# First-layer weights as the stationary operand in the expert tiles of a one-core metaformer kernel

## The chip, the cores and the metric

One Trainium2 chip, one core. The metric is the device time in microseconds (us) of one execution. Engines: PE (TensorE; its weight loads are written PEld), DVE (VectorE), ACT (ScalarE), POOL (GpSimd), SP (SyncE, which only issues DMAs here).

## What is computed

The input is 8 images of 64 channels and 16 x 16 pixels. Two blocks follow each other: deformable convolution and LSTM, then deformable convolution and a mixture of experts. The change touches the last part alone:

```
logits = flat @ router_w.T                      # 2048 tokens, 8 experts, the best 2 are taken
h = silu(flat @ w1[e].T) * (flat @ w3[e].T)     # 64 channels -> 682 hidden units
y = h @ w2[e].T                                 # 682 -> 64
out = sum over the two experts of gate * y
```

## The kernel before, in words

The 4096 pairs of token and expert are sorted by expert into 39 tiles of 128 rows (NT = 39); a tile has one expert, whose number the PE reads into a register. 16-bit operands are split into a high and a low float16 part, so each product is two matmuls.

- **POOL** gathers a tile's 128 rows from DRAM with an indirect DMA (fetch, L1195), seven tiles ahead, and scatters a tile's results with another (spread, L1202). In its loop fetch of tile t + 7 stands before spread of tile t, and spread waits for the row sums of DVE.
- **PE** turns the tokens (turn_tokens, L721): high and low parts of the 64 channels lie on 128 partitions. ACT copies that to `xts` (L1087).
- **first** (L724 to L739): for w1 (m = 0) and for w3 (m = 1), two halves of 341 hidden units times two parts. The stationary operand is `xts`, the moving one 341 columns of the weights at an address that hangs on the expert's register, so tokens are on partitions in the result. Eight matmuls a tile.
- ACT applies SiLU to the w1 result (gated, L1095); DVE multiplies it with the w3 result into `htok`, 128 tokens x 682 units of float32 (gated, L1688).
- **turn_hidden** (L741 to L750): six float32 transposes bring the units of `htok` onto partitions, into two banks of PSUM.
- ACT casts these banks to the high float16 part (high, L1104, two pieces), DVE subtracts to get the low part (low, L1697, two pieces).
- **second** (L752 to L767): twelve matmuls, six blocks of 128 units times two parts; the moving operand is w2 at a register address, which both parts of a block share. DVE adds the two halves of the result (rows_out, L1703).

The PE's order is written by hand (L775 to L784): in step t it does first(t), turn_tokens(t + 1), turn_hidden(t - 1), second(t - 2). ACT's order is gated(t), turned_tokens(t + 1), high(t - 1); DVE's is gated(t), low(t - 1), rows_out(t - 2). All waits are semaphores between engines. After the last spread the results are read back, weighted, turned (L787), added and stored.

Of the kernel before, what the change touches and what calls it, by code (L numbers as in the profile page):

```python
# [20 lines left out]
F32 = mybir.dt.float32  # L21
F16 = mybir.dt.float16
# [8 lines left out]
BQ = B // 2  # L31
# [63 lines left out]
def build(nc, x, consts, conv_w, conv_b, sample_w, bn, lstm_u, lstm_v, lstm_b, router, w13, w2, out):  # L95
    with ExitStack() as ctx:
# [3 lines left out]
        def sem(name):  # L100
            return ctx.enter_context(nc.semaphore(name))

        duo = [ctx.enter_context(nc.psum_tensor(f"duo{i}", [P, 1024], F32)) for i in range(2)]
        single = [ctx.enter_context(nc.psum_tensor(f"bank{i}", [P, 512], F32)) for i in range(4, 8)]
        bank = [duo[i // 2][:, i % 2 * 512:i % 2 * 512 + 512] for i in range(4)] + [b[:, :] for b in single]

        tent_c = sb("tent_c", [P, 2, 2, TAPS, 16])
# [93 lines left out]
        ytok = over(st0, 0, [P, 16 * 2 * C]).rearrange("p (g k n) -> p g k n", g=16, k=2)  # L202
        lsel = over(st1, 0, [P, 32 * TILE], F16).rearrange("p (c n) -> p c n", c=32)
        ybuf = over(st1, 0, [P, NP40 * C]).rearrange("p (t c) -> p t c", t=NP40)
        silu = over(st1, 2560, [P, 2 * HID]).rearrange("p (u n) -> p u n", u=2)
        xts = over(st1, 3924, [P, 3 * TILE], F16).rearrange("p (u n) -> p u n", u=3)
        hh = zw[0][:, :, :, :, :].rearrange("p a b c d -> p (a b c d)").rearrange("p (u n) -> p u n", u=3)
        hl = zw[1][:, :, :, :, :].rearrange("p a b c d -> p (a b c d)").rearrange("p (u n) -> p u n", u=3)
        htok = hid[:, :, :].rearrange("p a b -> p (a b)")[:, 0:2 * HP].rearrange("p (u n) -> p u n", u=2)
# [39 lines left out]
        for n in ("ld_const", "ld_mean", "ld_x", "ld_conv", "ld_lstm", "ld_w", "ld_late",  # L249
                  "zero", "bn_a", "bn_d",  # L250
                  "c_max", "c_tr", "c_pow", "c_bc", "c_scale",
                  "w_part", "w_max", "w_tr", "w_pow", "w_bc", "w_scale", "w_fac", "w_high", "w_low", "l_scaled",
                  "l_gi", "l_o", "l_act", "l_oact", "l_c", "l_tc", "l_h", "l_hc", "l_up", "l_res", "l_init", "l_zero", "r_half", "r_seed", "r_newton",
                  "e_pads", "e_conv", "e_om", "e_turn", "e_omt", "e_sig", "e_dist", "e_far", "e_tents", "e_tent",
                  "k_const", "x_turned", "x_centred", "x_square", "x_var", "x_sd", "x_rs", "m_log", "m_high", "m_low", "m_xrow", "m_exp",
                  "m_sm", "m_rank", "m_tot", "m_pos", "m_lane",
                  "m_tab", "m_zero",
                  "m_xtp", "m_xts", "m_h", "m_silu", "m_hid", "m_ht", "m_hh", "m_hl",
                  "m_y", "m_ys", "m_rows", "m_yld", "m_gate", "m_mix", "m_sum", "m_tr",
                  *[f"m_g{k}" for k in range(AHEAD)],  # L260
                  "m_out", "st_out"):
            s(n)
# [64 lines left out]

            return (slice(0, 8), slice(8, 12), slice(12, 16))[q]

        def halves_of(m):  # L330

            return duo[m][:, :].rearrange("p (h n) -> p h n", h=2)[:, :, 0:HID // 2]
# [61 lines left out]
        def _(pe):  # L394
# [321 lines left out]
            def turn_tokens(t):  # L716

                pe.wait_ge(s(f"m_g{t % AHEAD}"), 16 * (t // AHEAD + 1))
                if t > 0:
                    pe.wait_ge(s("m_xts"), t)  # L720
                nc.tensor.transpose(bank[4][:, 0:64].bitcast(F16), xg[:, t, :], ident16[:, :])\  # L721
                    .then_inc(s("m_xtp"), 1)

            def first(t):  # L724

                e = owner_of(t)

                n = HID // 2
                pe.wait_ge(s("m_xts"), t + 1)
                for m in range(2):  # L730
                    if t > 0:
                        pe.wait_ge(s(("m_silu", "m_hid")[m]), t)
                    for half in range(2):
                        for part in range(2):
                            at = 2 * SLOT + part * EW + m * HID + half * n
                            mm = nc.tensor.matmul(duo[m][:, half * 512:half * 512 + n], xts[:, t % 3, :],  # L736
                                                  w16[:, bass.ds(e * SLOT + at, n)],
                                                  start=(part == 0), stop=(part == 1))
                    mm.then_inc(s("m_h"), 1)  # L739

            def turn_hidden(t):  # L741

                pe.wait_ge(s("m_hid"), t + 1)
                for b in range(EB):
                    if t > 0 and b % 4 == 0:
                        pe.wait_ge(s("m_hl"), 2 * t - 1 + b // 4)
                    mm = nc.tensor.transpose(bank[6 + b // 4][:, b % 4 * 128:b % 4 * 128 + 128],  # L747
                                             htok[:, t % 2, b * 128:b * 128 + 128], ident[:, :])
                    if b in (3, EB - 1):
                        mm.then_inc(s("m_ht"), 1)  # L750

            def second(t):  # L752

                e = owner_of(t)

                if t > 0:
                    pe.wait_ge(s("m_ys"), t)
                for b in range(EB):
                    if b % 4 == 0:
                        pe.wait_ge(s("m_hl"), 2 * t + 1 + b // 4)  # L760
                    for part in (hh, hl):
                        mm = nc.tensor.matmul(bank[5][:, 0:2 * C],  # L762
                                              part[:, t % 3, b * 128:b * 128 + 128],
                                              w216[:, bass.ds(e * HP + (2 * HP + b * 128), 128)],
                                              start=(b == 0 and part is hh), stop=(b == EB - 1 and part is hl),
                                              skip_group_check=True)
                mm.then_inc(s("m_y"), 1)  # L767

            pe.wait_ge(s("m_tab"), 1)
            pe.wait_ge(s("w_low"), PAIRS * PAIRK)  # L770
            pe.wait_ge(s("m_zero"), 1)
            pe.wait_ge(s("m_high"), 4)
            loaded = [pe.value_load(words[0:1, k:k + 1], min_val=0, max_val=E ** TPW - 1) for k in range(WORDS)]
            turn_tokens(0)
            for t in range(NT + 2):  # L775
                if t < NT:
                    first(t)
                    if t + 1 < NT:
                        turn_tokens(t + 1)
                if 1 <= t <= NT:  # L780
                    turn_hidden(t - 1)
                if t >= 2:
                    second(t - 2)
            for j in range(8):  # L784
# [9 lines left out]
        def _(act):  # L794
# [287 lines left out]
            def turned_tokens(t):  # L1082

                act.wait_ge(s("m_xtp"), t + 1)
                if t >= 3:
                    act.wait_ge(s("m_h"), 2 * (t - 2))
                nc.scalar.copy(xts[:, t % 3, :], bank[4][:, 0:64].bitcast(F16))\  # L1087
                    .then_inc(s("m_xts"), 1)

            def gated(t):  # L1090

                act.wait_ge(s("m_h"), 2 * t + 1)
                if t >= 2:
                    act.wait_ge(s("m_hid"), t - 1)
                nc.scalar.activation(silu[:, t % 2, :].rearrange("p (h n) -> p h n", h=2), halves_of(0), ACT.Silu, scale=wsc[:, 4:5])\  # L1095
                    .then_inc(s("m_silu"), 1)

            def high(t):

                if t >= 3:  # L1100
                    act.wait_ge(s("m_y"), t - 2)
                for k, (lo, hi) in enumerate(((0, 512), (512, HP))):
                    act.wait_ge(s("m_ht"), 2 * t + k + 1)
                    nc.scalar.copy(hh[:, t % 3, lo:hi], bank[6 + k][:, 0:hi - lo]).then_inc(s("m_hh"), 1)  # L1104

            turned_tokens(0)
            for t in range(NT + 1):
# [9 lines left out]
        def _(gp):  # L1117
# [66 lines left out]
            gp.wait_ge(s("c1_out_ps"), BQ)  # L1184
            gp.wait_ge(s("c1_sz_done"), NG * B)
            nc.gpsimd.memset(htok[:, :, HID:HP], 0.0).then_inc(s("m_zero"), 1)

            gp.wait_ge(s("m_xrow"), 16)
            gp.wait_ge(s("m_tab"), 2)

# [24 lines left out]
        def _(dve):  # L1215
# [466 lines left out]
            def gated(t):  # L1682
# [1 line left out]
                dve.wait_ge(s("m_silu"), t + 1)  # L1684
                dve.wait_ge(s("m_h"), 2 * t + 2)
                if t >= 2:
                    dve.wait_ge(s("m_ht"), 2 * t - 2)
                nc.vector.scalar_tensor_tensor(out=htok[:, t % 2, 0:HID].rearrange("p (h n) -> p h n", h=2),  # L1688
                                               in0=halves_of(1), scalar=wsc[:, 5:6],
                                               in1=silu[:, t % 2, :].rearrange("p (h n) -> p h n", h=2),  # L1690
                                               op0=ALU.mult, op1=ALU.mult).then_inc(s("m_hid"), 1)

            def low(t):

                for k, (lo, hi) in enumerate(((0, 512), (512, HP))):
                    dve.wait_ge(s("m_hh"), 2 * t + k + 1)
                    nc.vector.tensor_tensor(hl[:, t % 3, lo:hi], bank[6 + k][:, 0:hi - lo], hh[:, t % 3, lo:hi],  # L1697
                                            ALU.subtract).then_inc(s("m_hl"), 1)

            def rows_out(t):  # L1700

                dve.wait_ge(s("m_y"), t + 1)
                nc.vector.reduce_sum(ybuf[:, t, :], bank[5][:, 0:2 * C]  # L1703
                                     .rearrange("p (k c) -> p c k", k=2), AX.X).then_inc(s("m_ys"), 1)

            for t in range(NT + 2):
# [101 lines left out]
```

## Time and profile before

| | us |
|---|---|
| median of 3 runs | 826.81 (823.98 to 828.96) |
| the profiled execution | 822.92 |
| its span | 821.2 |
| first matmul of the first expert tile | 697.79 |
| last scatter of an expert tile issued | 804.29 |

Times within the span count from its start. A row of the timeline gives start, duration, engine, line, operation, output <- inputs, number, and in brackets how long the engine had been idle and what released it ("issue": it waited for nothing that the profile shows). A row of the groups by line gives busy us, mean ns of one, and the idle time before. "PEldq" in a row is the sequencer that issues weight loads and matmuls.

### The profile page before, as it was taken

How to read it: one execution, taken by the hardware profiler on the slowest of the kernel's cores; microseconds unless marked ns; L12 is line 12 of the kernel's file. 1: busy time of each engine (PE TensorE's matmuls, PEld its weight loads, DVE VectorE, ACT ScalarE, POOL GpSimd, SP SyncE). 2: the span in 40 equal slices, each digit the busy share in tenths (PEclk: the TensorE clock that was granted, in tenths of full speed). 3: DMA queues.
4: the chain of work that ended last, by engine and by line, in shares of the span. 5: the costliest groups of instructions: out<-in, count | busy, mean ns of one | idle time of the engine just before them, and what ended most of it. 6: DMA issues, size and time to landing. Idle time of an engine off the chain costs nothing.

```text
span 821.2 us, 16043 instructions
## 1 busy us (share of the span) xinstructions
PE 653.5 (80%) x5315; PEld 524.9 (64%) x5315; DVE 505.7 (62%) x1672; ACT 421.4 (51%) x1492; POOL 235.4 (29%) x209
## 2 busy tenths in 40 slices
PE   5799998666787667776689888976899961999991
PEld 3478787555566555655566656654788961788881
DVE  4688884456654566655434444344888878688883
ACT  3476775233333555553334444446677771677760
POOL 0587682000000000000002100000887601677751
PEclk9999999555555555555555555555899985899996
DMA  9910000000000000000000000000000000111112
GB/s 211 212 32 2 2 2 1 2 1 0 1 2 1 1 1 1 2 0 1 1 0 2 1 1 2 1 1 1 1 2 2 2 2 29 23 28 27 28 21 81
DMA packets 12769, 14.97 MB, mean 18 GB/s; under 512 B 5873, under 2 KB 8626, under 8 KB 12690
## 3 DMA queue, kind: packets, MB, share of 16 engines
q1 hardware_dynamic: 9906, 11.26, 6.1%
q0 software_dynamic: 2496, 2.56, 1.5%
q8 instruction: 45, 0.74, 0.4%
q14 instruction: 34, 0.28, 0.1%
q10 hardware_dynamic: 288, 0.13, 0.1%
HBM read 11.62 MB, written 2.33 MB: 17 GB/s over the span
## 4 chain that ended last, share of the span: by engine, by line
PE 58%; DVE 17%; ACT 13%; issue 8%; DMA 2%; DVEq 1%; SPq 1%; POOL 0%; POOLq 0%; ACTq 0%
PE bank L486 7%; DVE bank L1510 6%; PE duo L736 6%; PE duo L664 6%; PE bank L664 5%; DVE hr L1514 4%; PE bank L469 4%; ACT duo L1036 4%; PE duo L434 4%; ACT bank L1040 4%; PE duo L666 3%; PE bank L666 3%; PE bank L747 3%; PE bank L762 3%; PE duo L469 3%
## 5 line engine op out<-in xcount | busy, mean ns | idle before, releaser
L1143 POOL TENSOR_TENSOR st<-tent,tentx 128x768 f32<-128x768 f32 x72 | 112.5, 1592 | 172.9 <-DVE tentx L1284 123.5
L1510 DVE TENSOR_TENSOR_SCAN bank<-duo,scan_add 64x24 f32<-64x24 f32 x256 | 52.8, 206 | 125.4 <-ACT duo L1036 125.1
L1143 POOL TENSOR_TENSOR st<-sq 128x768 f32<-128x768 f32 x9 | 13.2, 1500 | 305.7 <-DVE sq L1499 305.7
L668 PE MATMUL bank<-hr,lv 64*64 64x8 f32 x512 | 91.5, 251 | 0.0
L664 PE MATMUL bank<-hr,lv 64*64 64x8 f32 x256 | 48.5, 261 | 51.5 <-DVE hr L1514 51.4
L664 PEld LDWEIGHTS bank<-hr,lv 64*64 64x64 f32 x256 | 36.3, 201 | 81.2 <-DVE hr L1514 81.1
L664 PE MATMUL duo<-hr,lv 64*64 64x8 f32 x256 | 48.5, 261 | 46.5 <-DVE hr L1514 46.2
L664 PEld LDWEIGHTS duo<-hr,lv 64*64 64x64 f32 x256 | 36.3, 201 | 76.3 <-DVE hr L1514 76.0
L1514 DVE SCALAR_TENSOR_TENSOR hr<-tog,bank 64x8 f32<-64x8 f32 x256 | 39.6, 155 | 73.4 <-ACT bank L1040 73.4
L668 PEld LDWEIGHTS bank<-hr,lv 64*64 64x64 f32 x512 | 84.4, 223 | 0.0
L486 PE MATMUL bank<-zw,shi 128*128 128x128 f16 x576 | 79.6, 220 | 1.1 <-ACT osb L880 0.8
L486 PE MATMUL bank<-zw,hid 128*128 128x128 f16 x576 | 79.6, 220 | 0.0
L1292 DVE SCALAR_TENSOR_TENSOR hid<-bank,shi 128x512 f16<-128x512 f32 x96 | 64.7, 686 | 18.5 <-ACT shi L870 17.9
L1036 ACT ACTIVATE duo<-duo 64x16 f32<-64x16 f32 x128 | 19.6, 153 | 102.1 <-PE duo L666 101.9
L870 ACT ACTIVATE shi<-bank 128x512 f16<-128x512 f32 x96 | 57.2, 596 | 28.2 <-PE bank L469 27.3
L1036 ACT ACTIVATE duo<-bank 64x16 f32<-64x16 f32 x128 | 19.6, 153 | 93.6 <-PE bank L666 93.4
L469 PE MATMUL bank<-ident,st 128*128 128x128 f32 x384 | 60.5, 282 | 1.6 <-DVE hid L1292 1.4
L486 PEld LDWEIGHTS bank<-zw,shi 128*128 128x128 f16 x576 | 56.7, 99 | 2.2 <-DVE hid L1292 1.9
L486 PEld LDWEIGHTS bank<-zw,hid 128*128 128x128 f16 x576 | 56.7, 98 | 1.6
L736 PE MATMUL duo<-w13s,st 128*128 x312 | 54.1, 318 | 1.3 <-ACT st L1087 1.3
L1040 ACT ACTIVATE bank<-bank 64x8 f32<-64x8 f32 x256 | 37.6, 147 | 29.7 <-DVE bank L1510 2.2
L1038 ACT ACTIVATE tog<-bank 64x8 f32<-64x8 f32 x256 | 43.8, 171 | 15.2
(257 smaller groups left out, 1564.4 us busy)
## 6 DMA issues: line engine op xcount, KB each, us to landing
w13s<-w SPq DMA_DIRECT2D x16, 320.0 KB
w2s<-w SPq DMA_DIRECT2D x4, 320.0 KB
st<-yrows SPq DMA_DIRECT2D x2, 512.0 KB, 4.6
st<-xrows,xidx POOLq DMA_INDIRECT x39, 2.5
yrows<-st,yidx POOLq DMA_INDIRECT x39, 2.2
samw<-sample_w SPq DMA_DIRECT2D x2, 288.0 KB, 4.2
xs<-x SPq DMA_DIRECT2D x2, 256.0 KB, 4.2
xrows<-st SPq DMA_DIRECT2D x1, 512.0 KB, 2.6
```

Source lines behind the costliest of these rows:

```text
L469: mm = nc.tensor.transpose(bank[3 + g % RING][:, k * 128:k * 128 + 128], st[m % 2][:, t, tap, half * 128:half * 128 + 128], ident[:, :])
L486: mm = nc.tensor.matmul(bank[6][:, lo:lo + 2 * C], part[:, place(p, h), k, :], zw[p][:, half, tap, :, :].rearrange("p k c -> p (k c)"), st ...
L664: nc.tensor.matmul(both[:, 0, t, :], lv[:, C:2 * C], prev, start=False, stop=True, skip_group_check=True)
L668: nc.tensor.matmul(go, lv[:, 2 * C:3 * C], prev, start=False, stop=True, skip_group_check=True).then_inc(s("l_o"), 1)
L736: mm = nc.tensor.matmul(duo[m][:, half * 512:half * 512 + n], xts[:, t % 3, :], w16[:, bass.ds(e * SLOT + at, n)], start=(part == 0), stop ...
L870: nc.scalar.activation(shi[:, place(m % 2, g), :, :].rearrange("p k n -> p (k n)"), bank[3 + g % RING][:, :], ACT.Copy, scale=SSCALE / (1 ...
L1036: nc.scalar.activation(gate_in[:, 1:3, :], both, ACT.Tanh).then_inc(s("l_act"), 1)
L1040: nc.scalar.activation(tcell[:, :], cell[:, :, 2], ACT.Tanh, scale=0.5).then_inc(s("l_tc"), 1)
L1143: nc.gpsimd.tensor_tensor(st[p][:, t, k:k + KG, :].rearrange("p k (y x) -> p k y x", x=16), ty, tx, ALU.mult)\
L1292: nc.vector.scalar_tensor_tensor(out=slo[:, place(m % 2, g), :, :].rearrange("p k n -> p (k n)"), in0=bank[3 + g % RING][:, :], scalar=SSC ...
L1510: nc.vector.tensor_tensor_scan(cell[:, :, :].rearrange("p b k -> p (b k)"), gates, scan_add[:, :, :].rearrange("p b k -> p (b k)"), 0.0, A ...
L1514: nc.vector.scalar_tensor_tensor(out=hr[:, n % (2 * W), :], in0=tog[:, :], scalar=1.0, in1=tcell[:, :], op0=ALU.add, op1=ALU.mult).then_in ...
```

## The change

The operands of the first layer trade places: 128 columns of the weights are loaded into the array, and `xts` (128 columns) is streamed. The result has hidden units on partitions, six blocks of up to 128 units side by side (the sixth has 42), so the transposes of turn_hidden go, with their two banks. The w1 result alternates between two pairs of banks (gate_half). SiLU, product, cast and subtraction work on 128 x 768 instead of 128 x 682, and cast and subtraction are one instruction each, reading `htok` in SBUF instead of banks of PSUM. The memset of the padding of `htok` on POOL (L1186) goes, with the PE's wait for it (L771). The cut diff:

```
-        duo = [... f"duo{i}", [P, 1024] ... for i in range(2)]
+        duo = [... f"duo{i}", [P, 1024] ... for i in range(3)]
...
-        silu = over(st1, 2560, [P, 2 * HID]) ...
+        silu = over(st1, 2560, [P, 2 * HP]) ...
...
+        def gate_half(t):
+            return duo[t % 2 * 2]
...
             def first(t):
                 e = owner_of(t)
-                n = HID // 2
                 pe.wait_ge(s("m_xts"), t + 1)
                 for m in range(2):
-                    if t > 0:
-                        pe.wait_ge(s(("m_silu", "m_hid")[m]), t)
-                    for half in range(2):
+                    to = duo[1] if m else gate_half(t)
+                    if m == 0 and t > 1:
+                        pe.wait_ge(s("m_silu"), t - 1)
+                    elif m == 1 and t > 0:
+                        pe.wait_ge(s("m_hid"), t)
+                    for b in range(EB):
+                        n = 128 if b < FT else REST
                         for part in range(2):
-                            at = 2 * SLOT + part * EW + m * HID + half * n
-                            mm = nc.tensor.matmul(duo[m][:, half * 512:half * 512 + n], xts[:, t % 3, :],
-                                                  w16[:, bass.ds(e * SLOT + at, n)],
+                            at = 2 * SLOT + part * EW + m * HID + b * 128
+                            mm = nc.tensor.matmul(to[0:n, b * 128:b * 128 + 128],
+                                                  w16[:, bass.ds(e * SLOT + at, n)], xts[:, t % 3, :],
                                                   start=(part == 0), stop=(part == 1))
                     mm.then_inc(s("m_h"), 1)
-            def turn_hidden(t):
-                pe.wait_ge(s("m_hid"), t + 1)
-                for b in range(EB):
-                    if t > 0 and b % 4 == 0:
-                        pe.wait_ge(s("m_hl"), 2 * t - 1 + b // 4)
-                    mm = nc.tensor.transpose(bank[6 + b // 4][:, b % 4 * 128:b % 4 * 128 + 128],
-                                             htok[:, t % 2, b * 128:b * 128 + 128], ident[:, :])
-                    if b in (3, EB - 1):
-                        mm.then_inc(s("m_ht"), 1)
             def second(t):
...
-                    if b % 4 == 0:
-                        pe.wait_ge(s("m_hl"), 2 * t + 1 + b // 4)
+                    if b == 0:
+                        pe.wait_ge(s("m_hl"), t + 1)
+                    n = 128 if b < FT else REST
                     for part in (hh, hl):
-                        mm = nc.tensor.matmul(bank[5][:, 0:2 * C],
-                                              part[:, t % 3, b * 128:b * 128 + 128],
-                                              w216[:, bass.ds(e * HP + (2 * HP + b * 128), 128)],
+                        mm = nc.tensor.matmul(bank[7][:, 0:2 * C],
+                                              part[0:n, t % 3, b * 128:b * 128 + 128],
+                                              w216[0:n, bass.ds(e * HP + (2 * HP + b * 128), 128)],
...
-            pe.wait_ge(s("m_zero"), 1)
...
-                if 1 <= t <= NT:
-                    turn_hidden(t - 1)
...
             def gated(t):                                   (ACT)
-                nc.scalar.activation(silu[...], halves_of(0), ACT.Silu, scale=wsc[:, 4:5])
+                nc.scalar.activation(silu[:, t % 2, :], gate_half(t)[:, 0:HP], ACT.Silu, scale=wsc[:, 4:5])
             def high(t):                                    (ACT)
-                for k, (lo, hi) in enumerate(((0, 512), (512, HP))):
-                    act.wait_ge(s("m_ht"), 2 * t + k + 1)
-                    nc.scalar.copy(hh[:, t % 3, lo:hi], bank[6 + k][:, 0:hi - lo]).then_inc(s("m_hh"), 1)
+                act.wait_ge(s("m_hid"), t + 1)
+                nc.scalar.copy(hh[:, t % 3, :], htok[:, t % 2, :]).then_inc(s("m_hh"), 1)
...
-            nc.gpsimd.memset(htok[:, :, HID:HP], 0.0).then_inc(s("m_zero"), 1)
...
             def gated(t):                                   (DVE)
                 if t >= 2:
-                    dve.wait_ge(s("m_ht"), 2 * t - 2)
+                    dve.wait_ge(s("m_hl"), t - 1)
+                nc.vector.scalar_tensor_tensor(out=htok[:, t % 2, :],
+                                               in0=duo[1][:, 0:HP], scalar=wsc[:, 5:6], in1=silu[:, t % 2, :],
+                                               op0=ALU.mult, op1=ALU.mult).then_inc(s("m_hid"), 1)
             def low(t):                                     (DVE)
+                dve.wait_ge(s("m_hh"), t + 1)
+                nc.vector.tensor_tensor(hl[:, t % 3, :], htok[:, t % 2, :], hh[:, t % 3, :], ALU.subtract)\
+                    .then_inc(s("m_hl"), 1)
```

## Rows read from the trace of the kernel before

**Rows 1.** The page: busy time of each engine, and the granted TensorE clock in 40 slices.
```profile
PE 653.5 (80%) x5315; PEld 524.9 (64%) x5315; DVE 505.7 (62%) x1672; ACT 421.4 (51%) x1492; POOL 235.4 (29%) x209
...
PEclk9999999555555555555555555555899985899996
```
**Rows 2.** Busy time of each engine in a stretch of the expert tiles, then clock, DMA.
```profile
740.00:760.00 20.00, 20.00 (x215) 17.07 (x212) 16.49 (x32) 14.49 (x32) 15.25 (x16) 1.00 0.13 27
```
**Rows 3.** The chain that ended last (start, us, what): first tile, one steady tile.
```profile
697.79 2.46 PE duo L736 x8
...
740.68 1.17 PE duo L736 x8
741.90 0.66 PE bank L747 x6
742.56 0.67 PE bank L762 x12
```
**Rows 4.** Groups by line and shape, 690 to 800 us: DVE in the expert tiles.
```profile
L1688 DVE SCALAR_TENSOR_TENSOR hid<-duo,wsc,st 128x682 f32<-128x682 f32 x39 | 36.2, 928 | 23.0 <-ACT st L1095 16.4 <-PE duo L736 6.6
...
L1697 DVE TENSOR_TENSOR zw<-bank,zw 128x512 f16<-128x512 f32 x38 | 26.3, 691 | 0.5 <-ACT zw L1104 0.4
...
L1697 DVE TENSOR_TENSOR zw<-bank,zw 128x256 f16<-128x256 f32 x38 | 15.8, 415 | 0.0
L1703 DVE TENSOR_REDUCE st<-bank 128x64 f32<-128x128 f32 x36 | 10.1, 281 | 0.0
```
**Rows 5.** Timeline of POOL: the first, the 32nd and the last scatter.
```profile
708.52 1.01 POOL L1202 DMA_INDIRECT yrows<-st,yidx  x1 [4.51 <-DVE st L1703]
...
788.39 0.99 POOL L1202 DMA_INDIRECT yrows<-st,yidx  x1 [0.30 <-issue]
...
804.29 0.97 POOL L1202 DMA_INDIRECT yrows<-st,yidx  x1 [0.42 <-DVE st L1703]
```
**Rows 6.** Source lines 736 and 762: sequencer's address instructions (ns min/median/max, first and last start).
```profile
L736 PEldq FUSED_REGOPS  x312: 46/46/65, 697.7 to 797.5; - x156
...
L762 PEldq FUSED_REGOPS  x234: 46/46/60, 706.0 to 803.3; - x117
```
**Rows 7.** Timeline of the weight loads in narrow stretches: first layer, then second layer.
```profile
743.18 0.10 PEld L736 LDWEIGHTS duo<-w13s,st 128*128 128x128 f16 x1
...
743.31 0.10 PEld L736 LDWEIGHTS duo<-w13s,st 128*128 128x128 f16 x1
...
743.68 0.10 PEld L736 LDWEIGHTS duo<-w13s,st 128*128 128x128 f16 x1
...
802.77 0.11 PEld L762 LDWEIGHTS bank<-w2s,zw 128*128 128x128 f16 x2 [1.36 <-issue]
...
802.89 0.11 PEld L762 LDWEIGHTS bank<-w2s,zw 128*128 128x128 f16 x2
```
**Rows 8.** From a wait's end to the first matmul: chain at 697, timeline at 802.
```profile
697.44 0.35 issue
...
802.34 0.28 DVE L1703 TENSOR_REDUCE st<-bank 128x64 f32<-128x128 f32 x1
802.77 0.73 PEld L762 LDWEIGHTS bank<-w2s,zw 128*128 128x128 f16 x12 [1.36 <-issue]
```
**Rows 9.** Timeline of PE: the first layer of the third and of the 39th tile.
```profile
704.30 1.33 PE L736 MATMUL duo<-w13s,st 128*128 x8
...
796.74 1.34 PE L736 MATMUL duo<-w13s,st 128*128 x8
```
**Rows 10.** Groups by line and shape, 660 to 680 us: a float32 minus float16 in SBUF.
```profile
L1627 DVE TENSOR_TENSOR st<-sq,st 128x512 f16<-128x512 f32 x2 | 1.4, 688 | 0.7 <-ACT st L1077 0.7
```
**Rows 11.** Timeline, 694 to 696 us: the first two gathers, and DVE beside the first.
```profile
694.06 1.18 POOL L1195 DMA_INDIRECT st<-xrows,xidx  x1 [24.46 <-DVE yidx L1667]
694.13 0.42 DVE L1673 TENSOR_TENSOR spare<-xc 128x256 f32<-128x256 f32 x1
...
695.54 0.95 POOL L1195 DMA_INDIRECT st<-xrows,xidx  x1 [0.30 <-issue]
```

More of the change, by code:

```diff
@@ L101, in sem @@
             return ctx.enter_context(nc.semaphore(name))
-        duo = [ctx.enter_context(nc.psum_tensor(f"duo{i}", [P, 1024], F32)) for i in range(2)]
-        single = [ctx.enter_context(nc.psum_tensor(f"bank{i}", [P, 512], F32)) for i in range(4, 8)]
-        bank = [duo[i // 2][:, i % 2 * 512:i % 2 * 512 + 512] for i in range(4)] + [b[:, :] for b in single]
+        duo = [ctx.enter_context(nc.psum_tensor(f"duo{i}", [P, 1024], F32)) for i in range(3)]
+        single = [ctx.enter_context(nc.psum_tensor(f"bank{i}", [P, 512], F32)) for i in range(6, 8)]
+        bank = [duo[i // 2][:, i % 2 * 512:i % 2 * 512 + 512] for i in range(6)] + [b[:, :] for b in single]
         tent_c = sb("tent_c", [P, 2, 2, TAPS, 16])
@@ L204, in build @@
         ybuf = over(st1, 0, [P, NP40 * C]).rearrange("p (t c) -> p t c", t=NP40)
-        silu = over(st1, 2560, [P, 2 * HID]).rearrange("p (u n) -> p u n", u=2)
-        xts = over(st1, 3924, [P, 3 * TILE], F16).rearrange("p (u n) -> p u n", u=3)
+        silu = over(st1, 2560, [P, 2 * HP]).rearrange("p (u n) -> p u n", u=2)
+        xts = over(st1, 4096, [P, 3 * TILE], F16).rearrange("p (u n) -> p u n", u=3)
         hh = zw[0][:, :, :, :, :].rearrange("p a b c d -> p (a b c d)").rearrange("p (u n) -> p u n", u=3)
@@ L256, in build @@
                   "m_sm", "m_rank", "m_tot", "m_pos", "m_lane",
-                  "m_tab", "m_zero",
-                  "m_xtp", "m_xts", "m_h", "m_silu", "m_hid", "m_ht", "m_hh", "m_hl",
+                  "m_tab",
+                  "m_xtp", "m_xts", "m_h", "m_silu", "m_hid", "m_hh", "m_hl",
                   "m_y", "m_ys", "m_rows", "m_yld", "m_gate", "m_mix", "m_sum", "m_tr",
@@ L328, in token_rows @@
             return (slice(0, 8), slice(8, 12), slice(12, 16))[q]
-        def halves_of(m):
-            return duo[m][:, :].rearrange("p (h n) -> p h n", h=2)[:, :, 0:HID // 2]
+        def gate_half(t):
+            return duo[t % 2 * 2]
         code16 = code[:, :, :].rearrange("p k g -> p (k g)").bitcast(F16)
@@ L720, in turn_tokens @@
                     pe.wait_ge(s("m_xts"), t)
-                nc.tensor.transpose(bank[4][:, 0:64].bitcast(F16), xg[:, t, :], ident16[:, :])\
+                nc.tensor.transpose(bank[6][:, 0:64].bitcast(F16), xg[:, t, :], ident16[:, :])\
                     .then_inc(s("m_xtp"), 1)
@@ L1086, in turned_tokens @@
                     act.wait_ge(s("m_h"), 2 * (t - 2))
-                nc.scalar.copy(xts[:, t % 3, :], bank[4][:, 0:64].bitcast(F16))\
+                nc.scalar.copy(xts[:, t % 3, :], bank[6][:, 0:64].bitcast(F16))\
                     .then_inc(s("m_xts"), 1)
@@ L1094, in gated @@
                     act.wait_ge(s("m_hid"), t - 1)
-                nc.scalar.activation(silu[:, t % 2, :].rearrange("p (h n) -> p h n", h=2), halves_of(0), ACT.Silu, scale=wsc[:, 4:5])\
+                nc.scalar.activation(silu[:, t % 2, :], gate_half(t)[:, 0:HP], ACT.Silu, scale=wsc[:, 4:5])\
                     .then_inc(s("m_silu"), 1)
@@ L1183, in _ @@
             conv(1)
-            gp.wait_ge(s("c1_out_ps"), BQ)
-            gp.wait_ge(s("c1_sz_done"), NG * B)
-            nc.gpsimd.memset(htok[:, :, HID:HP], 0.0).then_inc(s("m_zero"), 1)
             gp.wait_ge(s("m_xrow"), 16)
@@ L1686, in gated @@
                 if t >= 2:
-                    dve.wait_ge(s("m_ht"), 2 * t - 2)
-                nc.vector.scalar_tensor_tensor(out=htok[:, t % 2, 0:HID].rearrange("p (h n) -> p h n", h=2),
-                                               in0=halves_of(1), scalar=wsc[:, 5:6],
-                                               in1=silu[:, t % 2, :].rearrange("p (h n) -> p h n", h=2),
+                    dve.wait_ge(s("m_hl"), t - 1)
+                nc.vector.scalar_tensor_tensor(out=htok[:, t % 2, :],
+                                               in0=duo[1][:, 0:HP], scalar=wsc[:, 5:6], in1=silu[:, t % 2, :],
                                                op0=ALU.mult, op1=ALU.mult).then_inc(s("m_hid"), 1)
             def low(t):
[L1695 to L1698, printed above, removed]
+                dve.wait_ge(s("m_hh"), t + 1)
+                nc.vector.tensor_tensor(hl[:, t % 3, :], htok[:, t % 2, :], hh[:, t % 3, :], ALU.subtract)\
+                    .then_inc(s("m_hl"), 1)
             def rows_out(t):
                 dve.wait_ge(s("m_y"), t + 1)
-                nc.vector.reduce_sum(ybuf[:, t, :], bank[5][:, 0:2 * C]
+                nc.vector.reduce_sum(ybuf[:, t, :], bank[7][:, 0:2 * C]
                                      .rearrange("p (k c) -> p c k", k=2), AX.X).then_inc(s("m_ys"), 1)
```

## The prediction, made before the run

> **What bounds the kernel now.** I read the page first, then the busy time by stretch, the chain of waits, and last the timelines of single engines. The page [rows 1] says that PE is the busiest engine, but its share is an average over stages, so the stage of the expert tiles has to be read for itself. In it [rows 2] PE is busy 20.00 of 20 us at the full clock, the 2.4 GHz level; DVE, ACT and POOL show gaps. The chain [rows 3] runs through PE alone there: 1.17 us for the eight matmuls of the first layer, 0.66 us for the six turns, 0.67 us for the twelve matmuls of the second layer, and some 0.06 us for the token turn. That is 2.56 us a tile. From the third tile to the 39th [rows 9] it is (796.74 - 704.30) / 36 = 2.568 us.
>
> Two other resources lie right under that bound. POOL alternates a gather and a scatter without a real wait: from the first scatter to the 32nd [rows 5] it takes (788.39 - 708.52) / 31 = 2.576 us a pair. The other is the PE's sequencer, which no share of busy time shows. Each new register address of a matmul is one address instruction: 312 / 39 = 8 a tile in the first layer, 234 / 39 = 6 in the second, where the two parts share one [rows 6]. Such an instruction lasts 46 ns, but what counts is the distance. Where nothing else holds the sequencer, the weight load behind the next new address starts 0.12 to 0.13 us after the last one, with one matmul for each address (743.18, 743.31, and three addresses on 743.68) and with two (802.77, 802.89) [rows 7]. Twelve second-layer loads from an empty queue, with six addresses, take 0.73 us [rows 8], again 0.12 us an address. Over four addresses it is (743.68 - 743.18) / 4 = 0.125 us; the starts are rounded to 0.01, and I take 0.124. In the first layer of the kernel before this is hidden: a matmul of 341 columns holds the array for 1.17 / 8 = 0.146 us, longer than an address.
>
> **The change part by part.** Sizes are per tile.
>
> The array: 24 matmuls of 128 columns replace eight of 341. A pair of load and matmul of 128 columns takes 0.67 / 12 = 0.056 us [rows 3], so 24 x 0.056 = 1.34 us replace 1.17. The six turns save 0.66 us. Second layer and token turn stay. The array would need 37 x 0.056 = 2.07 us instead of 2.56.
>
> DVE: the product grows from 682 to 768 columns. The two subtractions [rows 4] give a slope of (691 - 415) / 256 = 1.08 ns a column, so the product costs 928 + 86 x 1.08 = 1021 ns. The subtraction becomes one instruction with both inputs in SBUF; the nearest row is the same operation at 512 columns, 688 ns [rows 10], so 688 + 256 x 1.08 = 964 ns against 691 + 415 = 1106. With the row sums of 281 ns that is 2.27 us, 0.05 less than before. ACT, busy 14.49 of 20 us [rows 2], changes as little: one SiLU that is an eighth wider, one cast instead of two. Neither binds.
>
> Addresses: in the loop of the first layer each block, part and layer has its own constant, so 24 matmuls need 24 new addresses instead of eight; the second layer keeps six. The sequencer's time is 30 x 0.124 = 3.72 us, and what stands between: from the end of a wait through the expert's shift and mask to the first matmul 0.35 us, from the wait on the row sums to the second layer's first load 802.77 - 802.62 = 0.15 us [rows 8], the token turn 0.06 us. In all 4.28 us. The same sum for the kernel before is 14 x 0.124 + 0.56 = 2.30 us, and that it lies under 2.56 is why no wait of that kind shows today. So the array no longer sets the pace: the sequencer does, at 4.28 us.
>
> What the trace doesn't show is an address on the weight load; before, it stands on the streamed operand. Below, it can cost nothing more than an address on a matmul, as two matmuls per address cost no more than one [rows 7]. A gain is not excluded, and the lower end is that the new addresses hide completely, which is the first rival. Above, the weight load of 0.10 us could fall out of the overlap. I take no extra cost, since in the rows the sequencer goes on 0.12 us after an address whatever follows it.
>
> Waits: the w1 result now waits for the SiLU of two tiles ago, easier than before. The w3 result still waits for the product of the tile before; behind it on the PE's queue stand the token turn and the second layer. At 4.28 us a tile the product of 1.02 us is done while PE issues a token turn, a second layer and twelve addresses, some 2.4 us. The cast now waits for the product itself (behind it on ACT stands the next SiLU), and the second layer for the whole subtraction (behind it on PE the next first layer). Product, cast and subtraction take about 1.0 + 0.9 + 1.0 us, the cast by its two pieces in the room ACT has now, and have more than one tile's time. Cover for DVE, ACT and POOL (2.57 us a tile) is the sequencer; if that cover is gone, POOL is late next. The memset on POOL and PE's wait for it are costed at nothing: PE waits there for the table of owners anyway, and POOL for the index of the first gather [rows 11].
>
> The clock: at the lower level, 1.2 GHz, as in the first tile (2.46 us for eight matmuls instead of 1.17, in a slice with a granted clock of half [rows 1, 3]), 37 pairs would take about 2.1 x 2.07 = 4.3 us, as long as the sequencer needs. So even a fall of the clock adds at most some tenths here and there.
>
> The sum: tiles three to 38 are 36 x (4.28 - 2.568) = 61.6 us more. The first two tiles have no second layer; each takes (704.30 - 697.79) / 2 = 3.25 us now [rows 3, 9], of which 2.46 are matmuls, and 24 x 0.124 = 2.98 us in their place make 0.5 us more each, 1.0 us together. At the end one first layer of 2.98 instead of 1.34 us [rows 9] and no turns (0.66 us off) add 1.0 us. 61.6 + 1.0 + 1.0 = 63.6 us. The profiled execution would go from 822.92 to 886.5 us. The median of the runs shown, 826.81, is 3.9 us above that execution; on its scale I get 890.4 us.
>
> **The rivals.** *Faster, POOL bound.* If the sequencer doesn't hold the new addresses back, the array's 2.07 and DVE's 2.27 us are below POOL's 2.576, and POOL sets the end. After the 32nd scatter at 788.39 the last seven follow at 1.29 us, so the last one is at 797.4 instead of 804.29 [rows 5]: 6.9 us less, 819.9 us. For it: the sequencer isn't visible in the chain today. Against it: the spacing of 0.12 us in rows 7. It would need an address to cost under (2.576 - 0.56 - 0.74) / 24 = 0.053 us; from there on the forecast turns round.
>
> *Slower, the weight load exposed.* If a load at a register address isn't overlapped, 24 x 0.095 = 2.3 us a tile come on top: 38 x 2.3 = 87 us, 977 us. For it: nothing; the trace has no such load. Against it: loads with a fixed address behind an address instruction start on time.
>
> *Slower, POOL blocked.* The new subtraction has both inputs in SBUF. The first gather, 1.18 us, lies beside such a DVE operation of 0.42 us, the next ones, 0.95 us, don't show it [rows 11]. If a gather or scatter waited out the whole subtraction, POOL's pair would be 2.58 + 0.96 = 3.54 us. That stays under the 4.28 us of the forecast, so it decides only if the addresses are hidden: then 31 x 0.96 - 6.9 = 22.9 us slower, 849.7 us. The Trainium skill has this rule (SBUF — State Buffer, Who interferes with whom): a VectorE instruction with two SBUF inputs contends with a GpSimd instruction that reads SBUF. By that rule the rival holds where the faster one would; the 0.23 us on one gather neither proves nor excludes it.
>
> *No change.* An address at 0.053 to 0.06 us gives the present pace; nothing points to such a value.
>
> **How the numbers follow.** Forecast, sequencer bound at 4.28 us: 0.82. Faster, POOL bound: 0.08. Weight load exposed: 0.06. POOL blocked: 0.02. No change: 0.02. So faster by over 0.5% is 0.08, within 0.5% (about what a measurement of this kernel can tell) 0.02, slower 0.82 + 0.06 + 0.02 = 0.90. The likeliest case alone reaches from 880 to 900 us: twice the 5 us by which the runs shown differ, to either side. For what a load at a register address may cost beyond that, the range takes in a quarter of the exposed load, 22 us. It is 878 to 912 us.
>
> **What would show it.** Right: PE's busy share in the stage falls to about half, first-layer weight loads stand 0.12 us apart, tiles follow at about 4.3 us, address instructions are 936 for the first layer, PE's idle time there is put down to "issue" and not to an engine, and POOL's scatters wait for DVE by 1.7 us. The turns' 39 x 0.66 us are gone and nothing is gained. Wrong: loads at 0.056 us, with POOL back to back at 2.58 us; or first-layer pairs at 0.2 us or more; or PE waiting for the product or the subtraction.

## The result, and the profile after

The kernel after takes 900.58 us (median of 6 runs, 896.87 to 902.56), the kernel before 827.67 us (823.98 to 828.96, 6 runs beside them): a ratio of 1.0894 [1.0865, 1.0922], 72.9 us slower. The profiled execution took 902.56 us with a span of 899.3. The forecast was 890.4 us, in a range of 878 to 912: the sign and the mechanism came out, the size was 10 us short.

The page of the kernel after, its rows on the engines and on the granted clock, beside [rows 1]:

```profile
PE 724.9 (81%) x5705; PEld 558.5 (62%) x5705; DVE 510.2 (57%) x1633; ACT 423.3 (47%) x1453; POOL 235.2 (26%) x208
...
PEclk9899997555555555555555555599995599999995
```

PE's share rises from 80 to 81%, which tells nothing. The stretch of the expert tiles says more (busy us and, in brackets, instructions of PE, PEld, DVE, ACT, POOL, then clock, DMA share, GB/s), beside [rows 2]:

```profile
740.00:760.00 20.00, 19.53 (x165) 13.65 (x164) 8.77 (x13) 8.49 (x13) 9.28 (x10) 1.00 0.07 17
```

PE still looks full, at the full clock, the 2.4 GHz level. But 165 matmuls in 20 us are one in 0.121 us. A busy time made of matmuls that are pipelined into each other can't tell whether the array or its sequencer is the limit; the count and the distance can. DVE, ACT and POOL fall to between 53 and 61% of their busy time before, since tiles come more slowly. The chain of waits between 754 and 766 us (start, us, what), beside [rows 3]:

```profile
755.57 0.16 PE bank L721
755.73 0.97 PE bank L755 x12
756.71 0.10 issue
756.81 3.24 PE duo L739 x24
```

A tile is 0.16 + 0.97 + 0.10 + 3.24 = 4.47 us, all of it on PE. The first layer alone went from 1.17 to 3.2 us. The rows of its source line (ns min/median/max, first and last start), beside [rows 6]:

```profile
L739 PEldq FUSED_REGOPS  x936: 46/46/65, 703.7 to 876.0; - x188
L739 PEld LDWEIGHTS duo<-st,w13s x936: 94/96/152, 703.8 to 876.1; 128*128 x156, 128*42 x32
```

There is one address instruction for each load, 936 = 39 x 24 instead of 312, as forecast. The distance between loads, from the timeline of the weight loads in three narrow stretches of one first layer, beside [rows 7]:

```profile
788.71 0.10 PEld L739 LDWEIGHTS duo<-st,w13s 128*128 x1
...
788.83 0.10 PEld L739 LDWEIGHTS duo<-st,w13s 128*128 x1
...
789.03 0.10 PEld L739 LDWEIGHTS duo<-st,w13s 128*128 x1
```

0.12 us is the forecast distance; the 0.20 behind it, from the seventh load of the tile to the eighth, is one of the pauses that the forecast lacked (below). DVE's groups between 720 and 870 us, beside [rows 4]:

```profile
L1673 DVE SCALAR_TENSOR_TENSOR hid<-duo,wsc,st 128x768 f32<-128x768 f32 x34 | 34.6, 1018 | 73.5 <-PE duo L739 73.5
L1680 DVE TENSOR_TENSOR zw<-hid,zw 128x768 f16<-128x768 f32 x34 | 32.6, 958 | 4.2 <-ACT zw L1093 0.5
L1686 DVE TENSOR_REDUCE st<-bank 128x64 f32<-128x128 f32 x34 | 9.6, 283 | 0.0
```

Forecast were 1021, 964 and 281 ns. DVE waits for PE for 73.5 us in this stretch. The timeline of PE, first layers of the first three tiles, and POOL's first, 32nd and last scatter, beside [rows 9] and [rows 5]:

```profile
703.83 3.32 PE L739 MATMUL duo<-st,w13s 128*128 128x128 f16 x24 [0.67 <-ACT st L1077]
...
708.05 3.29 PE L739 MATMUL duo<-st,w13s 128*128 128x128 f16 x24 [0.68 <-ACT st L1077]
...
712.21 3.33 PE L739 MATMUL duo<-st,w13s 128*128 128x128 f16 x24 [0.65 <-ACT st L1077]
...
873.11 3.18 PE L739 MATMUL duo<-st,w13s 128*128 128x128 f16 x24
```

```profile
718.26 1.01 POOL L1187 DMA_INDIRECT yrows<-st,yidx  x1 [8.12 <-DVE st L1686]
...
856.58 0.98 POOL L1187 DMA_INDIRECT yrows<-st,yidx  x1 [2.24 <-DVE st L1686]
...
882.52 0.97 POOL L1187 DMA_INDIRECT yrows<-st,yidx  x1 [1.08 <-DVE st L1686]
```

From these the time between the two profiled executions can be laid out, span 899.3 against 821.2:

| stretch | before | after | difference | forecast |
|---|---|---|---|---|
| up to the first tile's first layer | 697.79 | 703.83 | +6.04 | 0 |
| two tiles | 6.51 | 8.38 | +1.87 | +1.0 |
| 36 tiles, third to 39th | 92.44 | 160.90 | +68.46 | +61.6 |
| from there to the last scatter | 7.55 | 9.41 | +1.86 | +1.0 |
| rest | 16.91 | 16.78 | -0.13 | 0 |

The first line is in stages that the diff leaves alone, and it moves among the runs that leave them alone too (the first address of the first tile is at 700.0 us in e2 and at 702.6 in e6). Without it the difference is 72.06 us, as by the medians (72.9).

### The profile page after: what moved, and what is told of

Same layout as the page of the kernel before. It is cut to its first block, busy times and chain, and to the rows that moved or that the text cites. A ratio compares the mean times of both kernels' runs of the same rounds, so it can differ in the third digit from the quotient of the medians.

```text
span 899.3 us, 17327 instructions
## 1 busy us (share of the span) xinstructions
PE 724.9 (81%) x5705; PEld 558.5 (62%) x5705; DVE 510.2 (57%) x1633; ACT 423.3 (47%) x1453; POOL 235.2 (26%) x208
## 4 chain that ended last, share of the span: by engine, by line
PE 59%; DVE 18%; ACT 12%; issue 8%; DMA 2%; DVEq 1%; POOL 0%; SPq 0%; POOLq 0%; ACTq 0%
PE duo L739 14%; PE duo L664 10%; PE duo L666 6%; PE duo L469 5%; DVE bank L1495 5%; PE bank L486 5%; PE duo L434 4%; PE bank L755 4%; DVE hr L1499 4%; ACT duo L1026 4%; ACT bank L1030 4%; PE duo L630 2%; DVE hid L1277 2%; PE duo L456 1%; DVE dist L1255 1%
## 5 line engine op out<-in xcount | busy, mean ns | idle before, releaser
L664 PE MATMUL duo<-hr,lv 64*64 64x8 f32 x512 | 97.1, 261 | 98.1 <-DVE hr L1499 97.6
L664 PEld LDWEIGHTS duo<-hr,lv 64*64 64x64 f32 x512 | 72.9, 202 | 157.6 <-DVE hr L1499 157.2
L739 PE MATMUL duo<-st,w13s 128*128 128x128 f16 x936 | 125.4, 236 | 5.6 <-ACT st L1077 2.0
L739 PEld LDWEIGHTS duo<-st,w13s 128*128 x936 | 88.6, 98 | 43.5 <-issue 14.4
L1277 DVE SCALAR_TENSOR_TENSOR hid<-duo,shi 128x512 f16<-128x512 f32 x144 | 95.7, 686 | 29.8 <-ACT shi L860 29.0
L860 ACT ACTIVATE shi<-duo 128x512 f16<-128x512 f32 x144 | 85.7, 596 | 55.3 <-PE duo L469 54.3
L469 PE MATMUL duo<-ident,st 128*128 128x128 f32 x576 | 90.9, 282 | 4.0 <-DVE hid L1277 3.7
L666 PE MATMUL duo<-hr,lv 64*64 64x8 f32 x512 | 91.6, 251 | 0.0
L1673 DVE SCALAR_TENSOR_TENSOR hid<-duo,wsc,st 128x768 f32<-128x768 f32 x39 | 39.7, 1018 | 88.2 <-PE duo L739 88.2
L666 PEld LDWEIGHTS duo<-hr,lv 64*64 64x64 f32 x512 | 84.8, 224 | 0.0
L469 PEld LDWEIGHTS duo<-ident,st 128*128 128x128 f32 x576 | 63.0, 143 | 14.6 <-issue 11.5
L1187 POOL DMA_INDIRECT yrows<-st,yidx x39 | 38.8, 996 | 95.0 <-DVE st L1686 95.0
```

Source lines behind the costliest of these rows:

```text
L469: mm = nc.tensor.transpose(bank[3 + g % RING][:, k * 128:k * 128 + 128], st[m % 2][:, t, tap, half * 128:half * 128 + 128], ident[:, :])
L664: nc.tensor.matmul(both[:, 0, t, :], lv[:, C:2 * C], prev, start=False, stop=True, skip_group_check=True)
L666: nc.tensor.matmul(both[:, 1, t, :], lv[:, 0:C], prev, start=False, stop=True, skip_group_check=True).then_inc(s("l_gi"), 1)
L739: mm = nc.tensor.matmul(to[0:n, b * 128:b * 128 + 128], w16[:, bass.ds(e * SLOT + at, n)], xts[:, t % 3, :], start=(part == 0), stop=(part ...
L860: nc.scalar.activation(shi[:, place(m % 2, g), :, :].rearrange("p k n -> p (k n)"), bank[3 + g % RING][:, :], ACT.Copy, scale=SSCALE / (1 ...
L1277: nc.vector.scalar_tensor_tensor(out=slo[:, place(m % 2, g), :, :].rearrange("p k n -> p (k n)"), in0=bank[3 + g % RING][:, :], scalar=SSC ...
```

## The experiments

**Which resource: addresses taken away.** `e1_fixed_first` is the kernel after with the weights of expert 0 in every tile, so that the first layer has fixed addresses:

```
-                                                  w16[:, bass.ds(e * SLOT + at, n)], xts[:, t % 3, :],
+                                                  w16[:, at:at + n], xts[:, t % 3, :],
```

> The changed kernel with the first layer's 24 matmuls a tile on the weights of expert 0, at fixed addresses, so that the 24 address instructions of a tile go; the choice of the expert in the first layer is left out, all other work stays. Theory (the address instructions hold PE's sequencer): the sequencer needs under 2 us a tile, the pace passes to POOL's 2.58 us a pair, and the time falls from about 900 to about 820 us, just under the kernel before. Rival (small matmuls with the weights as the stationary operand are slow in themselves, or their loads are not overlapped): about 900 us stay. Rival (POOL blocked by the subtraction with two SBUF inputs): about 850 us.

Measured: 835.75 us (833.53 to 838.88) beside 826.12 of the kernel before, ratio 1.0120 [1.0085, 1.0156]. So some 63 of the 72.9 us hang on the 24 address instructions of a tile and on nothing else that the change does. But the time is 15 us above what was expected: without the addresses the kernel is still slower than before. Its chain:

```profile
749.07 1.77 PE duo L739 x24
750.84 0.16 PE bank L721
751.00 0.83 PE bank L755 x12
```

That is 1.77 + 0.16 + 0.83 = 2.76 us on PE, where 2.07 had been priced: 24 pairs take 1.77 us and not 24 x 0.056 = 1.34. The timeline of PE in two narrow stretches, around the last blocks of the w1 result:

```profile
752.27 0.38 PE L739 MATMUL duo<-st,w13s 128*128 128x128 f16 x2
...
752.42 0.29 PE L739 MATMUL duo<-st,w13s 128*42 128x128 f16 x2
...
752.64 0.29 PE L739 MATMUL duo<-st,w13s 128*128 128x128 f16 x2
```

From the last matmul of 128 columns of weights to the first of 42 are 0.15 us, and from there to the next one of 128, two pairs later, 0.22. Pairs of one size follow at 0.056. There are six such changes a tile (into and out of the sixth block for w1, for w3 and in the second layer); at (1.77 - 1.34) / 4 = 0.11 us more for each they would raise 2.07 to some 2.7. What POOL does at the same time made a second suspect: its gathers last 1.2 us there instead of 0.97.

**Fewer addresses, more addresses.** `e2_shared` is the kernel after with both parts of a block at the high part's address (the low part of the weights is not used), 12 addresses instead of 24. `e3_before_six_more` is the kernel before with an address of its own for each part of the second layer, 20 a tile instead of 14:

```
e2:
-                            at = 2 * SLOT + part * EW + m * HID + b * 128
+                            at = 2 * SLOT + m * HID + b * 128
e3:
-                                              w216[:, bass.ds(e * HP + (2 * HP + b * 128), 128)],
+                                              w216[:, bass.ds(e * HP + (2 * HP + b * 128 + (0 if part is hh else 64 if b < FT else -32)), 128)],
```

> The changed kernel with both parts of a block at the address of the high part, so that 24 matmuls share 12 addresses a tile; the low part of the first layer's weights is left out. Theory: 12 address instructions less, 4.47 - 12 x 0.124 - 0.04 = 2.94 us a tile against 2.57 before, so about 842 us. Rival (loads or matmuls, whose number stays): about 900 us.

> The kernel before with six more address instructions a tile: in the second layer the low part takes its weights from columns shifted by 64 (by -32 in the last block), so both parts no longer share an address; the low part of the hidden units is multiplied by wrong columns. All matmuls keep their sizes. Theory: the sequencer, just under the array so far, goes to 20 x 0.124 + 0.7 + some 0.15 for pauses = 3.3 us a tile, 36 x 0.73 = 26 us more, about 854 us. Rival (the array bounds and addresses are hidden): 828 us as before.

Measured: `e2_shared` 841.67 us (840.67 to 843.26), ratio 1.0187 [1.0163, 1.0211]; `e3_before_six_more` 853.34 us (851.38 to 854.77), ratio 1.0317 [1.0290, 1.0345]. Both came within 1 us of what was expected. The second is the stronger: the kernel before keeps its operands' shapes, its engines' work and its waits (the low part of the second layer takes other columns of w2), only six address instructions a tile are added, and 27 us come. Its chain:

```profile
763.11 0.06 PE bank L721
763.17 0.66 PE bank L747 x6
763.83 0.93 PE bank L762 x12
764.75 0.36 issue
765.12 1.34 PE duo L736 x8
```

Beside [rows 3] the turns are as they were (0.66 us). The second layer went from 0.67 to 0.93 us, the first from 1.17 to 1.34, and 0.36 us of idle time stand between them that nothing but the sequencer accounts for.

**More loads at the same addresses.** `e6_twice` does every first-layer matmul twice (so the first layer's results are doubled), 48 pairs behind 24 addresses:

```
+                            for twice in range(2):
                                 mm = nc.tensor.matmul(...)
```

> The changed kernel with every first-layer matmul issued twice at the same address (accumulated, so the first layer's results are doubled): 48 loads and matmuls for the same 24 addresses. Theory: an address instruction's 0.124 us cover two pairs as well as one; only pauses every so many instructions grow, about 0.05 to 0.1 us a tile: 902 to 905 us. Rival (the weight loads or matmuls set the pace): 24 x 0.056 us a tile more at least, about 950 us.

Measured: 903.23 us (903.20 to 903.63), ratio 1.0928 [1.0907, 1.0949]. 936 more pairs of load and matmul add 0.0034 to the ratio of the kernel after, which is within the two intervals; as a time it would be 2.8 us, or 0.003 us a pair. The weight load isn't exposed, and the array isn't the bound in the kernel after. The rows of its source line, and its loads from the sixth address of a tile to the eighth:

```profile
L740 PEld LDWEIGHTS duo<-st,w13s x1872: 95/98/157, 702.7 to 878.8; 128*128 x156, 128*42 x32
...
L740 PEldq FUSED_REGOPS  x936: 46/46/65, 702.6 to 878.6; - x188
```

```profile
763.27 0.11 PEld L740 LDWEIGHTS duo<-st,w13s 128*128 x2
...
763.39 0.11 PEld L740 LDWEIGHTS duo<-st,w13s 128*128 x2
...
763.56 0.11 PEld L740 LDWEIGHTS duo<-st,w13s 128*128 x2
```

With two pairs behind each address the distance is still 0.12 us, and the pause (0.17) stands at the same place as in the kernel after, ahead of the eighth address.

**What holds the kernel once addresses are free.** Four kernels beside 25 runs of the kernel before (824.84 us). `e4_before_fixed_first` gives the kernel before fixed first-layer addresses, as e1 does for the kernel after:

> The kernel before, with the eight matmuls of the first layer on fixed addresses (always the weights of expert 0), so that 6 of its 14 address instructions a tile are left. Theory (before is held by the array at 2.56 us and by POOL at 2.576 us a tile, its sequencer lies under that): nothing changes, 824 to 830 us. Rival (the sequencer already held the kernel before): 8 x 0.124 = 0.99 us a tile less to issue, the time falls by at least 10 us.

Measured: 823.75 us (821.21 to 825.45), ratio 0.9984 [0.9963, 1.0005]. Eight addresses fewer bring nothing that can be told from no change: in the kernel before the sequencer lies under the array and POOL, as the forecast read it. Which of these two holds it, no run separates.

`e7_fixed_no_narrow` is e1 with all blocks 128 wide, in both layers (the sixth block of w1 and w3 then also multiplies 86 columns of other weights):

```
-                        n = 128 if b < FT else REST
+                        n = 128
```

> The kernel after with the first layer on fixed addresses, as in e1_fixed_first, and all blocks 128 wide, so that no matmul of 42 columns or rows is left (the sixth block of w1 and w3 also multiplies 86 columns that belong to others). e1 ran at 2.76 us a tile. Theory (the array held e1, since each of six changes between 128 and 42 a tile costs 0.09 us more than a pair): the array falls to about 2.1 us, POOL's pair stands alone, 2.58 us, and the time is 818 to 826 us. Rival 1 (pairs with weights as the stationary operand are slow in themselves): 834 to 838 us. Rival 2 (POOL held e1, because gathers wait out the subtraction): 830 to 836 us with gathers of 1.1 us.

`e9_narrow_one_input` is e1 with the subtraction replaced (the low part is not computed, a copy of `htok` stands in its place), `e8_no_narrow_one_input` has both edits:

```
-                nc.vector.tensor_tensor(hl[:, t % 3, :], htok[:, t % 2, :], hh[:, t % 3, :], ALU.subtract)\
+                nc.vector.tensor_scalar(hl[:, t % 3, :], htok[:, t % 2, :], 1.0, None, ALU.mult)\
```

> As e1_fixed_first (42-wide blocks kept), with the subtraction turned into a product of one input with 1.0 (the low part is not computed). Theory (the array at 2.75 us holds e1 by itself): gathers fall to 0.95 to 0.98 us, the time stays at 833 to 838 us. Rival (POOL's lengthened gathers hold e1): the time falls to 820 to 828 us.

> As e7_fixed_no_narrow, and the subtraction becomes a product with 1.0 of the one input htok (the low part is then not computed; DVE reads one tensor of SBUF there). Theory (array at about 2.1 us, gathers no longer lengthened): POOL's pair is 2.58 us with gathers of 0.95 to 0.98 us, 817 to 822 us. If gathers don't care for the second input, they stay as in e7 and so does the time.

| run | 42-wide blocks | subtraction | us | ratio |
|---|---|---|---|---|
| e1 (beside 826.12 us) | yes | two inputs | 835.75 | 1.0120 [1.0085, 1.0156] |
| e9 | yes | one input | 834.67 | 1.0101 [1.0040, 1.0162] |
| e7 | no | two inputs | 824.83 | 1.0008 [0.9985, 1.0030] |
| e8 | no | one input | 820.64 | 0.9959 [0.9934, 0.9985] |

With the 42-wide blocks the DVE edit changes nothing that the intervals can tell; without the blocks 9 to 14 us go (e1 to e7, e9 to e8). So the changes of size held e1, not POOL, and pairs with weights as the stationary operand are not slow in themselves. The chain of e9 repeats one tile without any idle time:

```profile
756.63 1.77 PE duo L739 x24
758.40 0.16 PE bank L721
758.56 0.77 PE bank L755 x12
```

That is 2.70 us of array. In e9 the gathers last 1.05 us, not the 0.95 to 0.98 that were expected: they don't start inside the one-input operation, but it starts 0.37 us into them (753.84 and 754.21). The chain of e7 over a ring that it repeats:

```profile
746.51 1.02 DVE hid L1673
747.52 0.86 DVE zw L1680
748.39 0.21 DVE st L1686
748.60 0.34 issue
748.94 0.90 PE bank L755 x12
749.85 0.76 PE duo L739 x12
750.61 0.02 issue
750.63 0.91 ACT st L1085
751.54 0.03 issue
751.57 1.02 DVE hid L1673
```

Twelve first-layer matmuls take 0.76 us, and the array no longer sets the pace: the chain is a ring over DVE, PE and ACT, 751.57 - 746.51 = 5.06 us for two tiles, 2.53 a tile. POOL's pair, with some gathers longer, is (794.98 - 710.68) / 31 = 2.72 us between its first and its 32nd scatter, but its last scatters wait for DVE; which of the two holds e7, these runs don't separate. The expectation had POOL alone. In e8 the chain of the same stretch is POOL's, gather and scatter back to back:

```profile
748.70 0.99 POOL yrows L1187
749.68 0.30 issue
749.99 1.17 POOL st L1180
```

The 4.2 us from e7 to e8 can come from the shorter DVE operation in the ring or from shorter gathers; this stays open too. Even with free addresses and no narrow block the new order is worth nothing (e7), and 4.2 us where the low part isn't computed either (e8); and here the expert of a tile is known only at run time, so that the addresses hang on a register. No version that computes the whole and beats the kernel before came out of these runs.

**Gathers and the subtraction.** The timelines of e7 and of the kernel before, a gather that starts while a subtraction runs. e7, DVE, then POOL:

```profile
749.61 0.95 DVE L1680 TENSOR_TENSOR zw<-hid,zw 128x768 f16<-128x768 f32 x1
```

```profile
749.68 1.72 POOL L1180 DMA_INDIRECT st<-xrows,xidx  x1 [0.30 <-issue]
```

Before, DVE, then POOL:

```profile
750.71 1.02 DVE L1697 TENSOR_TENSOR zw<-bank,zw 128x512 f16<-128x512 f32 x2
```

```profile
751.14 0.97 POOL L1195 DMA_INDIRECT st<-xrows,xidx  x1 [0.30 <-issue]
```

In e7 the gather ends at 751.40, 0.84 us after the subtraction's end at 750.56, and lasts 1.72 instead of 0.97 us. In e1 the 20 gathers from 743.64 to 797.01 all start inside a subtraction, and all end 0.84 to 0.85 us after it. Four earlier ones (the first at 715.66) start within 0.04 us of the subtraction's start and keep their 0.97 us. In the kernel before, where the subtraction reads a bank of PSUM and one tensor of SBUF, a gather that starts inside one takes its 0.97 us. In e8 the one-input operation, 0.55 us long, does it as well:

```profile
749.77 0.55 DVE L1680 TENSOR_SCALAR zw<-hid 128x768 f16<-128x768 f32 x1
```

It ends at 750.32, and the gather that began at 749.99 ends at 751.16, again 0.84 later. So the expectation of e8 was half right: the time is in its range, but an operation with one input holds a gather too, it only ends sooner.

## Why the prediction was right or wrong

**What bounds it: right.** The array or POOL held the kernel before, and the sequencer lay close under them: e4 shows that taking eight addresses away brings nothing, e3 that six more bring 27 us. A resource without a share of busy time was the next bound.

**24 new addresses at 0.124 us: right as the distance, too low as the price.** 936 address instructions, loads 0.12 apart, and the cost doesn't hang on what follows an address (e6). What the distance leaves out is the next point. A load at a register address costs as much as a matmul at one, so the value taken between the two bounds holds.

**The sum of a tile, 4.28 us: 0.19 too low.** The term that was short is 30 x 0.124 = 3.72 us; it measured 3.91, or 0.130 an address. The tile takes 160.90 / 36 = 4.47 us. The starts of the address instructions in 35 tiles say where it goes. Within a layer the distance is 0.124 us (0.138 behind the first address), except at three places: ahead of the eighth, the 16th and the 24th address of the first layer it is 0.134 to 0.279, in each of the 35 tiles. These pauses are 0.052 us on average, 0.16 us a tile. A fourth stands between the layers, where the distance from the last address of the second layer to the next first layer is 0.454 us on average and 0.423 where no pause falls on it (e2): 0.03 more. Without the four pauses the tile would be 4.28 us: what stands between, 0.56 us, was priced right, and it is the pauses that were put at nothing. Over 36 tiles that is 6.9 of the 72.06 - 63.6 = 8.5 us that were missing. The first two tiles and the end have the rest, 0.9 us each. In the two tiles most of it is in first layers of 3.3 us where 2.98 was priced; at the end most is in the last second layer, 1.57 us at 880.35 under a granted clock of 0.50, where the kernel before took 0.90 us at 802.78 under 1.00.

The rows of four and six addresses from which 0.124 was read are too short for a pause that comes once in eight. That it goes by the count, and neither by time nor by the matmuls, the places show: they stay the same while tiles last from 4.3 to 4.6 us, and in e6 they are the same with 48 pairs behind the 24 addresses (0.20 us a tile there for the three in the first layer). With the two instructions for the expert's shift and mask a tile of the kernel after has 32 of the sequencer's register instructions, four times eight; e2 has 20, and there the places alternate between two tiles. What the sequencer does in a pause, and why one lasts 0.01 us and another 0.15, stays open.

**DVE and ACT: right.** 1018, 958 and 283 ns against 1021, 964 and 281. PE waits for neither, as forecast.

**Waits: right.** POOL's scatters wait for DVE's row sums by 2.1 to 2.3 us, which is 4.47 - 2.58 = 1.9 us of slack and the 0.30 us that stand before every scatter [rows 5]; 1.7 was forecast with the shorter tile. The turns' time is gone from the chain and gained nothing.

**The clock: right.** By its row it was half, the 1.2 GHz level, up to some 719 us. The first layers in it took 3.29 to 3.33 us, the last one, at the full clock, 3.18. Between 832 and 834 us it was 0.50 once more; the two tiles around that, from 828.32 to 837.21, took 4.45 us each on average, no more than the others.

**The array at 2.07 us, and with it the faster rival's 819.9 us: wrong, without weight in the sum.** The price of 0.056 us a pair was that of twelve equal pairs. The change also brings pairs of 42, and each change of size costs 0.15 us instead of 0.056 (e1, gone in e7). Had the addresses been free, the kernel would have been at 835.75 us (e1), slower than before by 1.2%: the rival that was to end on the faster side would not have.

**POOL blocked: the mechanism is there, the price was too high.** A gather does wait for the subtraction. The Trainium skill (SBUF — State Buffer, Who interferes with whom) says that a VectorE instruction with two SBUF inputs contends with a GpSimd instruction that reads SBUF, and that a VectorE instruction in a two-port mode, which a `tensor_scalar` can enter, and GpSimd shut each other out, the first to issue holding the shared ports for its whole length. The trace agrees: 1.72 us for a gather of 0.97 in e7 and 1.17 in e8; that the operation of e8 ran in such a mode is not shown. But a gather waits for what is left of the operation, not for all of it, and one that starts before it loses little or nothing (0.08 us in e9, nothing in e1). So 0.96 us on each was too much: the 37 gathers of e7 between 700 and 800 us last 1.03 us on average. In the kernel after no gather of the loop meets a subtraction, and each takes 0.97 us from the ninth on; one scatter near the end does (878.74) and takes 1.43 us.

**PE's busy share "falls to about half": wrong.** It stayed at 19.53 of 20 us, since each matmul is shown with some 0.22 us while they come every 0.12. So only 0.07 to 0.20 us a tile were left to be put down to "issue". The count in the same row had the answer.

## What to carry to other kernels

Count the sequencer's address instructions as a resource of their own: each new register address on an expert's weights cost 0.124 us here, and with pauses 0.130, whether one pair of load and matmul used it or two, so expert weights as a stationary operand of 128 columns instead of a moving one of 341 need three times as many. Price matmuls by rows of the same sequence of sizes, not of equal ones. Before trusting a gain, ask what stands directly under the bound: here POOL, the DVE ring and the sequencer all stood within 0.3 us of it, so that 0.5 us less on the array could give nothing even with every address free (e7).

## What the runs showed that was not expected

- A change between matmuls of 128 and of 42 columns (or rows) takes 0.15 us from start to start instead of 0.056, in each direction; six of them a tile made 2.70 us of array out of 2.07 (e9).
- The sequencer pauses once in eight of its register instructions, by 0.05 us on average, on top of a distance of 0.124 us. The place goes by the count: it is the same with one and with two pairs behind an address (e6).
- A gather that starts during a DVE operation whose inputs all lie in SBUF, and over 0.04 us after the operation's start, ends 0.84 us or a little more after that operation, up to 1.72 us long; beside an operation that reads PSUM and SBUF it keeps its 0.97 us.
